# Attention, recurrence and experts on one core: the residual sum and the tile's final scaling move from VectorE to ScalarE, with new instruction orders

## The reference

```python
x = x + linear_attention(cross_attention(x, cond))         # 16 heads of 8, softmax over heads
hs = recurrence(x, h0=cond)                                # a scan over the 128 time steps
#   fused = sigmoid([x_t, h] @ w_W + w_b); a, o = split(fused)
#   h = o * h + (1 - o) * tanh(x_t @ wx + wx_b + a * (h @ wh + wh_b))
x = x + top2_of_8_experts(hs)                              # relu(h @ w1)^2 @ w2, weighted by a softmax of two logits
```

## Time and profile before

| | |
|---|---|
| median of 3 runs | 385.31 us (384.47 to 385.41) |
| the profiled execution's own time | 384.91 us |
| its span, first to last instruction | 383.2 us |
| TensorE matmuls / weight loads busy | 366.7 us (96%) / 304.8 us (80%) |
| VectorE busy | 335.3 us (88%) |
| ScalarE busy | 271.9 us (71%) |
| GpSimd busy | 261.8 us (68%) |
| granted TensorE clock, mean | 0.999 of 2.4 GHz |

### The profile page before, as it was taken

The page is one execution under the profiler, slowest core; times in us unless marked ns, Lnnn a source line. Parts: engine busy times, 40 slices in busy tenths (PEclk is TensorE's granted clock), DMA queues, the critical chain, the costliest instruction groups (busy, mean ns, idle before and its releaser), DMA issues.

```text
span 383.2 us, 9266 instructions
## 1 busy us (share of the span) xinstructions
PE 366.7 (96%) x2532; PEld 304.8 (80%) x2532; DVE 335.3 (88%) x1223; ACT 271.9 (71%) x1040; POOL 261.8 (68%) x273
## 2 busy tenths in 40 slices
PE   3899999999999999999999999999999999999985
PEld 3588788667888888888888888888888888888774
DVE  2367888999999999999999999999999999998640
ACT  2555534447788888888888887878888888776662
POOL 3799134797777777777777777777777777776000
PEclk9999999999999999999999999999999999999999
DMA  7600000000000000000000000000000000000000
GB/s 213 214 2 0 3 0 3 0 2 1 9 8 9 9 9 9 8 9 8 9 8 9 9 8 9 7 10 7 9 9 8 10 12 11 8 9 7 9 7 15
DMA packets 7585, 6.76 MB, mean 18 GB/s; under 512 B 880, under 2 KB 6256, under 8 KB 7536
## 3 DMA queue, kind: packets, MB, share of 16 engines
q1 hardware_dynamic: 7104, 5.79, 4.9%
q10 hardware_dynamic: 432, 0.39, 0.4%
HBM read 4.09 MB, written 2.10 MB: 16 GB/s over the span
## 4 chain that ended last, share of the span: by engine, by line
DVE 54%; issue 15%; PE 8%; POOL 1%; ACT 1%; DVEq 1%; POOLq 0%
DVE kvs L1072 14%; DVE att L1081 8%; PE bank L390 6%; DVE mem L1130 5%; DVE h L1150 4%; DVE bank L1135 4%; DVE rden L1064 4%; DVE bank L1142 3%; DVE kvs L1050 3%; DVE bank L1031 2%; POOL qc L347 1%; DVE bank L1104 1%; DVE bank L1056 1%; PE bank L539 1%; DVE x1T L1088 1%
## 5 line engine op out<-in xcount | busy, mean ns | idle before, releaser
L347 POOL TENSOR_TENSOR qc<-kvs,qn 128x512 f32<-128x512 f32 x64 | 81.4, 1274 | 22.9 <-DVE kvs L1072 18.8
L335 POOL TENSOR_TENSOR kv<-kv,qkv 128x512 f32<-128x512 f32 x64 | 81.1, 1268 | 2.4
L1072 DVE TENSOR_TENSOR_SCAN kvs<-bank,kv 128x256 f32<-128x256 f32 x128 | 81.5, 659 | 0.1
L390 PEld LDWEIGHTS bank<-h,gwh 128*128 128x128 f32 x512 | 68.2, 191 | 16.4 <-DVE h L1150 14.3
L832 ACT ACTIVATE hid<-bank,gw 128x128 f32<-128x128 f32 x256 | 76.3, 372 | 0.7 <-PE bank L390 0.6
L390 PE MATMUL bank<-h,gwh 128*128 128x32 f32 x512 | 72.7, 265 | 1.2 <-DVE h L1150 1.1
L390 PE MATMUL bank<-w,hsq 128*128 128x128 f32 x512 | 71.4, 283 | 1.8 <-ACT hsq L840 1.8
L390 PE MATMUL bank<-w,h 128*128 128x512 f32 x128 | 70.2, 630 | 0.0
L390 PEld LDWEIGHTS bank<-w,hsq 128*128 128x128 f32 x512 | 62.2, 192 | 3.5 <-ACT hsq L840 2.9
L858 ACT ACTIVATE gt<-bank 128x64 f32<-128x64 f32 x128 | 30.3, 237 | 44.7 <-PE bank L390 43.5
L390 PE MATMUL bank<-h,whw 128*128 128x64 f32 x256 | 50.5, 279 | 0.0
(11 more groups left out here) (112 smaller groups left out, 730.2 us busy)
## 6 DMA issues: line engine op xcount, KB each, us to landing
out_dram<-res SPq DMA_DIRECT2D x32, 64.0 KB
XT<-in_x_t_dram SPq DMA_DIRECT2D x7, 256.0 KB, 6.1
w<-in_w_dram SPq DMA_DIRECT2D x2, 512.0 KB, 5.8
XT<-in_x_t_dram ACTq DMA_DIRECT2D x1, 256.0 KB, 3.8
aw<-in_aw_dram SPq DMA_DIRECT2D x1, 192.0 KB, 3.2
gwx<-in_gw_dram SPq DMA_DIRECT2D x1, 128.0 KB, 4.6
gwh<-in_gw_dram SPq DMA_DIRECT2D x1, 128.0 KB, 4.3
cwk<-in_cwk_dram ACTq DMA_DIRECT2D x1, 64.0 KB, 1.8
```

The costliest lines, as they stand in the source:

```text
L335: pool.tensor_tensor(kv[:, a * D:b * D, :].rearrange("p (d e) h -> p d e h", d=D // 2), kv[:, D * D + a:D * D + b, :].unsqueeze(2).broadca ...
L347: pool.tensor_tensor(qc[:, a:b, :, :], kvs[:, a * D:b * D, :].rearrange("p (d e) h -> p d e h", d=D // 2), qn[:, p, a:b, :].unsqueeze(2).b ...
L390: return pe.matmul(dst, w, rhs, start=start, stop=True, skip_group_check=True)
L1072: dve.tensor_tensor_scan(flat(kvs[:, a:b, :]), scan_mask, flat(kv[:, a:b, :]), 0.0, ALU.mult, ALU.add).then_inc(kv_sum, 1)
```

## The change

`residual` becomes two ScalarE instructions: `x1_bias` writes XTt + bao into bank OUT, columns 128 to 255, TensorE's projection adds onto it, and `x1_out` copies the sum to `x1T`, now four tiles deep. The rows of x1 are no longer kept: `x_rows_out` writes them, times the sum of the weights, into OUT, columns 0 to 127; TensorE adds the experts' products there; ScalarE's `finish` multiplies by `grec` into `res`. VectorE loses `residual` and `finish`. The diff, with the ramps' lists and unchanged stretches left out (in the ramps the same calls are reordered, `x_rows` and the first experts come later, the ramp's `inverses(2, 0)` replaces VectorE's `sum_heads(2, 1)` and `residual(0)`, `sum_heads(0, *)` moves up to right after tile 0's inverses, `add_dims(0, *)` back behind `query_sum(2)`, and 34 fillers become 29):

```diff
 attT = sb("attT", [P, TOK])
-x1T = sb("x1T", [P, 2, STEPS, B])
+x1T = sb("x1T", [P, 4, STEPS, B])
...
-return (QKV, ATT)[half] if is_last(t) else HID
+return (QKV, MEM)[half] if is_last(t) else HID
...
     sp.dma_start(out_d[t], res[:, p, :]).then_inc(out_done, 16)
-for t in range(2):
-    store(t, t)
-with sp.Fori(1, TILES // 2) as it:
-    for p in range(2):
-        store(2 * it + p, p)
+for t in range(TILES):
+    store(t, t % 2)
 sp.wait_ge(out_done, 16 * TILES)
 @block.gpsimd
...
     keys(0, 0)
-    queries(0, 0)
     outer(0, 0, 0)
     outer(0, 0, 1)
+    queries(0, 0)
     weigh(0, 0, 0)
     weigh(0, 0, 1)
-    add_halves(0)
     keys(1, 1)
     outer(1, 1, 0)
-    outer(1, 1, 1)
 def iteration(t, p, has):
     q = 1 - p
+    if has(0):
+        add_halves(t)
+    if has(1):
+        outer(t + 1, q, 1)
     if has(2):
         keys(t + 2, p)
         outer(t + 2, p, 0)
...
         queries(t + 1, q)
         weigh(t + 1, q, 0)
         weigh(t + 1, q, 1)
-        add_halves(t + 1)
-    if has(2):
-        outer(t + 2, p, 1)
...
         last = mm(context_bank(u)[:, j * (D + 1) * D:(j + 1) * (D + 1) * D], pT[:, u % 2, j * P:(j + 1) * P],
-                  vbd[:, GROUP * (u % QUADS) + j, :, :].rearrange("p d h -> p (d h)"))
+                  vbd[:, GROUP * (u % QUADS) + j, :, :].rearrange("p d h -> p (d h)"), start=j == 0)
     last.then_inc(c_ps, 1)
...
     pe.wait_ge(a_red, 2 * t + 2)
-    at_least(pe, x1_done, t)
-    at_least(pe, x1t_sb, t)
+    at_least(pe, aT_sb, t)
+    at_least(pe, xr_ok, t - 2)
     pe.transpose(ATT[:, 0:P], att[:, :, :].rearrange("p h e -> p (h e)"), ident[:, :]).then_inc(aT_ps, 1)
 def project_out(t):
     pe.wait_ge(aT_sb, t + 1)
-    mm(ATT[:, P:2 * P], awo[:, :], attT[:, :]).then_inc(p_ps, 1)
+    pe.wait_ge(xb_ok, t + 1)
+    at_least(pe, xr_ok, t - 1)
+    mm(OUT[:, P:2 * P], awo[:, :], attT[:, :], start=False).then_inc(p_ps, 1)
 def x_rows(t, p):
     pe.wait_ge(x1_done, t + 1)
-    pe.transpose(ATT[:, 2 * P:3 * P], x1T[:, p, :, :].rearrange("p l b -> p (l b)"), ident[:, :])\
+    pe.wait_ge(aT_sb, min(t + 3, TILES))
+    at_least(pe, xr_ok, t)
+    pe.transpose(ATT[:, 2 * P:3 * P], x1T[:, t % 4, :, :].rearrange("p l b -> p (l b)"), ident[:, :])\
         .then_inc(x1t_ps, 1)
 def gates_x(t, p):
-    xs = x1T[:, p, :, :].rearrange("p l b -> p (l b)")
+    xs = x1T[:, t % 4, :, :].rearrange("p l b -> p (l b)")
     if isinstance(t, int) and t == 0:
         pe.wait_ge(h_init, 2)
...
     pe.wait_ge(hsq_sb, 2 * t + half + 1)
-    if half == 0 and not is_last(t):
-        at_least(pe, res_done, NE * t)
+    if half == 0:
+        pe.wait_ge(xr_ok, t + 1)
+        pe.wait_ge(x1_done, min(t + 3, TILES))
     if t == 0:
         pe.wait_ge(c_sb, 2 * QUADS)
     for j in range(4):
-        last = mm(out_bank(t)[:, 0:C], hsq[:, half, j * P:(j + 1) * P], w2[:, 4 * half + j, :],
-                  start=half == 0 and j == 0)
+        last = mm(out_bank(t)[:, 0:C], hsq[:, half, j * P:(j + 1) * P], w2[:, 4 * half + j, :], start=False)
     last.then_inc(o_ps, 1)
...
 def iteration(t, p, has):
     q = 1 - p
     if has(0):
+        gates_x(t, p)
         memory_x(t, p)
         step_gates(t, p, 0)
-        step_memory(t, p, 0)
     if has(-1):
         logits(t - 1, q)
-        hidden(t - 1, q, 0)
+    if has(0):
+        step_memory(t, p, 0)
+    if has(-2):
+        experts_out(t - 2, 0)
+        hidden_T(t - 2, 1)
+    if has(0):
+        step_gates(t, p, 1)
+        step_memory(t, p, 1)
     if has(4):
         qkv_of(t + 4)
-    if has(0):
-        step_gates(t, p, 1)
-        x_rows(t, p)
-        step_memory(t, p, 1)
-    if has(-2):
-        hidden_T(t - 2, 1)
+    if has(-1):
+        hidden(t - 1, q, 0)
+    if has(0):
+        step_gates(t, p, 2)
+        step_memory(t, p, 2)
     if has(1):
         att_T(t + 1)
-    if has(-2):
-        experts_out(t - 2, 0)
-    if has(0):
-        step_gates(t, p, 2)
-        step_memory(t, p, 2)
     if has(-2):
         experts_out(t - 2, 1)
     if has(-1):
         hidden_T(t - 1, 0)
+        x_rows(t - 1, q)
+    if has(0):
+        step_gates(t, p, 3)
+        step_memory(t, p, 3)
     if has(1):
         project_out(t + 1)
-    if has(0):
-        step_gates(t, p, 3)
-        step_memory(t, p, 3)
     if has(-1):
         hidden(t - 1, q, 1)
-    if has(1):
-        gates_x(t + 1, q)
 def finale():
+    x_rows(31, 1)
     experts_out(30, 0)
...
+def x1_bias(t):
+    if t == 0:
+        act.wait_ge(c_sb, 2 * QUADS)
+    at_least(act, res_done, t - 3)
+    act.activation(OUT[:, P:2 * P], XTt[:, STEPS * t:STEPS * (t + 1), :], ACT.Identity, bias=bao).then_inc(xb_ok, 1)
+def x1_out(t, p):
+    act.wait_ge(p_ps, t + 1)
+    at_least(act, xz_done, t - 3)
+    at_least(act, x1t_ps, t - 3)
+    act.activation(x1T[:, t % 4, :, :].rearrange("p l b -> p (l b)"), OUT[:, P:2 * P], ACT.Copy).then_inc(x1_done, 1)
 def x_rows_out(t):
     act.wait_ge(x1t_ps, t + 1)
-    act.activation(x1[:, ds(t, 1), :].rearrange("p o c -> p (o c)"), ATT[:, 2 * P:3 * P], ACT.Copy)\
-        .then_inc(x1t_sb, 1)
+    act.wait_ge(gs_done, t + 1)
+    if not is_last(t):
+        at_least(act, res_done, t)
+    act.activation(out_bank(t)[:, 0:C], ATT[:, 2 * P:3 * P], ACT.Identity, scale=gsum[:, :]).then_inc(xr_ok, 1)
+def finish(t, p):
+    act.wait_ge(o_ps, 2 * t + 2)
+    act.wait_ge(gr_done, t + 1)
+    at_least(act, out_done, 16 * (t - 1))
+    act.activation(res[:, p, :], out_bank(t)[:, 0:C], ACT.Identity, scale=grec[:, p:p + 1]).then_inc(res_done, 1)
 def relu(t, p, half, some):
...
     act.wait_ge(gw_done, t + 1)
     at_least(act, gr_done, t)
+    at_least(act, xr_ok, t)
     act.activation(gw2[:, :], gw[:, p, :], ACT.Square, accum_out=gsum[:, :]).then_inc(gs_done, 1)
 def gate_exp(t, p):
...
 def iteration(t, p, has):
     q = 1 - p
     if has(-2):
+        relu(t - 2, p, 1, 0)
+    if has(0):
+        gates(t, p, 0)
+    if has(-2):
         relu(t - 2, p, 1, 1)
     if has(0):
-        gates(t, p, 0)
+        memory_tanh(t, 0)
     if has(4):
         qkv_bias(t + 4)
-    if has(0):
-        memory_tanh(t, 0)
     if has(3):
         exp_qk(t + 3, q)
     if has(0):
         gates(t, p, 1)
-        x_rows_out(t)
+    if has(-2):
+        square(t - 2, 1)
+    if has(0):
         memory_tanh(t, 1)
+    if has(-1):
+        gate_exp(t - 1, q)
+    if has(4):
+        qkv_out(t + 4, p)
+    if has(-1):
+        relu(t - 1, q, 0, 0)
+    if has(0):
+        gates(t, p, 2)
+    if has(-1):
+        relu(t - 1, q, 0, 1)
+    if has(0):
+        memory_tanh(t, 2)
     if has(1):
         att_out(t + 1)
     if has(-1):
-        gate_exp(t - 1, q)
+        taken_sum(t - 1, q)
     if has(-2):
-        square(t - 2, 1)
+        finish(t - 2, p)
+    if has(1):
+        x1_bias(t + 1)
     if has(-1):
-        relu(t - 1, q, 0, 0)
-    if has(0):
-        gates(t, p, 2)
-    if has(-1):
-        relu(t - 1, q, 0, 1)
-    if has(0):
-        memory_tanh(t, 2)
-    if has(-1):
-        taken_sum(t - 1, q)
-    if has(4):
-        qkv_out(t + 4, p)
-    if has(-1):
-        square(t - 1, 0)
+        x_rows_out(t - 1)
     if has(0):
         gates(t, p, 3)
     if has(1):
         gates_bias(t + 1)
+        x1_out(t + 1, q)
     if has(0):
         memory_tanh(t, 3)
     if has(1):
         memory_bias(t + 1)
     if has(-1):
-        relu(t - 1, q, 1, 0)
+        square(t - 1, 0)
 def finale():
...
-def residual(t, p):
-    dve.wait_ge(p_ps, t + 1)
-    at_least(dve, x1t_ps, t - 1)
-    at_least(dve, xz_done, t - 1)
-    dve.scalar_tensor_tensor(out=x1T[:, p, :, :],
-                             in0=ATT[:, P:2 * P].rearrange("p (l b) -> p l b", b=B),
-                             scalar=bao, in1=XTt[:, ds(STEPS * t, STEPS), :],
-                             op0=ALU.add, op1=ALU.add).then_inc(x1_done, 1)
 def largest_logits(t):
     dve.wait_ge(mask_ok, 2)
...
 def taken_inverse(t, p):
     dve.wait_ge(gs_done, t + 1)
+    at_least(dve, res_done, t - 1)
     dve.reciprocal(grec[:, p:p + 1], gsum[:, :]).then_inc(gr_done, 1)
-def finish(t, p):
-    dve.wait_ge(o_ps, 2 * t + 2)
-    dve.wait_ge(gr_done, t + 1)
-    dve.wait_ge(x1t_sb, t + 1)
-    at_least(dve, out_done, 16 * (t - 1))
-    dve.scalar_tensor_tensor(out=res[:, p, :], in0=out_bank(t)[:, 0:C], scalar=grec[:, p:p + 1],
-                             in1=x1[:, ds(t, 1), :].rearrange("p o c -> p (o c)"), op0=ALU.mult,
-                             op1=ALU.add).then_inc(res_done, NE)
 def memory(t, p, s):
...
 def iteration(t, p, has):
     q = 1 - p
     if has(0):
         memory(t, p, 0)
         renewed(t, 0)
+    if has(-1):
+        drop_others(t - 1)
+    if has(0):
+        kept(t, p, 0)
+        new_h(t, p, 0)
     if has(2):
-        inverses(t + 2, 0)
-    if has(0):
-        kept(t, p, 0)
-    if has(-1):
-        largest_logits(t - 1)
-    if has(0):
-        new_h(t, p, 0)
+        sum_heads(t + 2, 1)
     if has(1):
         add_dims(t + 1, 0)
+    if has(0):
+        memory(t, p, 1)
+        renewed(t, 1)
```

(131 more changed lines are left out.)

131 lines of the change are left out of this document (58 added, 73 removed).

## The result

The changed kernel takes 383.45 us (median) against 384.48 us in the runs beside it: ratio 0.996, 95% interval 0.9949 to 0.9971. It is faster, but by 1.0 us between the medians and 1.5 by the ratio, where I forecast 6.6. One of its 11 runs took 456.13 us at a granted clock of 0.757, and the ratio is taken without it.

| stretch, by the start of the instruction that gives `x1T` | before | after | change |
|---|---|---|---|
| start to the first `x1T` | 72.94 | 71.40 | -1.5 |
| the next two tiles | 18.12 | 17.88 | -0.2 |
| 26 steady tiles | 242.46 | 241.27 | -1.2 |
| the last three | 26.46 | 27.45 | +1.0 |
| from the last `x1T` to the end | 23.2 | 22.9 | -0.3 |

The account below looks back on a forecast made before the run. VectorE was taken to pace the kernel at 9.24 us a tile, TensorE next at 9.10. 384.91 - 4.3 (steady tiles) - 1.0 (first tiles) - 1.3 (ramp) = 378.3, or 378.7 against the median; range 374.8 to 383.6.

Parts of the forecast that it names:

- What bounds the kernel now: Old steady tile: VectorE paces it at 9.24 us of its own work, with TensorE needing only 9.10.
- TensorE's 9.10 as the next bound: Steady tiles: with VectorE down to about 8.8 us, TensorE's 9.10 us of work a tile sets the pace.
- Onto ScalarE: ScalarE's queue: 0.26 us for each of three new instructions, 0.09 for a scale column, 0.87 a tile.
- the new waits: TensorE, ScalarE and VectorE queues in steady tiles: the added waits cost nothing if ScalarE's pieces have the sizes assumed.
- rival C: ScalarE's three instructions before `gates(3)` take over 1.4 us, delaying the recurrence: slower, 387.6 us at the upper bound; chance 0.07.
- the 0.6 that I had named as a sign of being wrong: ScalarE, step 3: the forecast is wrong if `gates(3)` starts over 0.6 us after its `step_gates`.
- Steady tiles: 26 steady tiles: TensorE's 9.10 plus 0.06 for late VectorE instructions, 9.16 a tile, gains 4.3 us.
- Ramp: From 40 to 76 us: the reordered ramp gains 1.3 us, between -0.5 and 3.
- first tiles: First three tiles, with fillers on TensorE: a third of VectorE's relief counts, 1.0 us, bounds 0 and 1.7.
- the rule of the Trainium skill: Add and mul belong on VectorE; set aside because in these fp32 rows ScalarE is not the slower engine.
- B: Steady tiles: TensorE as good as full, stalls VectorE hid now show, only the start gains: 382.0 us; chance 0.21.
- A: Steady tiles: TensorE is no bound, all of VectorE's 0.58 us a tile comes through: 369.3 us; chance 0.04.

Follow-up runs that it names:

- rows_late: The changed kernel with ScalarE's `x_rows_out` moved from ahead of `gates(3)` to behind `memory_bias`, after the projection: 378.64 us, 0.987 of the changed kernel.
- bias_cheap: The changed kernel with `x1_bias` reading a contiguous block of XT and adding no bias (other numbers result): 379.19 us, ratio to before 0.9858.
- late_contig: The changed kernel with `x_rows_out` after the projection, plus `x1_bias` reading a contiguous block, bias column kept (other numbers result): 377.76 us, ratio 0.9814.
- before_logits2: The kernel before, its store loop written out, with the logits product issued twice on TensorE: 390.94 us, ratio 1.0154.

## Why the prediction was wrong, by its own steps

*What bounds the kernel now.* Half right. VectorE was full, and so, in effect, was TensorE. In the old order 0.26 less of VectorE is worth 0.065 in the usual tile (0.11 on average), and 0.23 more of TensorE costs 0.24. I read 9.10 of work out of a tile of 9.24 and called the rest air; the part at step 0 was a wait for h inside the loop, which a lighter VectorE did not remove.

*TensorE's 9.10 as the next bound.* Right in sum for the new order: rows_late runs at 9.10, and a small product added there costs all of its 0.23. The parts are less good. Its steps take 2.26, 2.21, 2.16 and 2.47 against my 2.20, 2.21, 2.27 and 2.42, and its `step_gates` 0.36 to 0.41 where I had 0.36 everywhere. The errors cancel, and that 9.10 came out to the hundredth is luck. The changed kernel itself does not get there.

*Onto ScalarE, and the new waits: these steps failed.* One term was mis-sized: I charged `x1_bias` 0.26 in the queue, of bounds 0.16 to 0.59, and it measured 0.40. For its stride I had taken nothing, with 0.06 as the bound; it is 0.12. And I asked of `project_out` only whether `x1_bias` was done. Its other wait, `at_least(pe, xr_ok, t - 1)`, in `project_out(t + 1)` asks for `x_rows_out(t - 1)`, issued in the same step, last of the three, and I never named it. "More than a step old" I had said of `att_T`, `x_rows` and the experts; of `x_rows` it was false too, since its wait on `aT_sb` is for the `att_out` of the same step, but that ends at 217.39, in time for 217.71. Nor had I counted that `x_rows_out` can't start before `x_rows` has ended.

It took both errors. With `x1_bias` at the 0.26 I gave, `x_rows_out` would have waited for `x_rows` as in bias_cheap, where the wait costs 0.04 a tile and the mean is 9.158, my 9.16 (an estimate, from that run's 0.28 between the two); with the wait on that `x_rows_out` gone, an `x1_bias` of 0.40 costs nothing (rows_late, late_contig). Together they cost the 0.16. Had I only named the wait, my own sizes would have passed it, with `x_rows_out` done in the queue by 2.64 and the projection due at 2.88.

I placed the danger at `gates(3)` (rival C), with 0.2 to spare. It starts 0.62 after its `step_gates`, past the 0.6 that I had named as a sign of being wrong, but 0.61 with ScalarE idle before it (rows_late): the sign was set too tight, and the three instructions, 0.96 together instead of 0.78, held up the projection and not `gates(3)`.

*Steady tiles.* Forecast 9.16, gain 4.3 us; measured 9.280, gain 1.2. Undone by rows_late: 9.117, under the forecast, since of the 0.06 that I kept for late instructions only some 0.02 was left.

*Ramp, first tiles.* 1.3 forecast and 1.5 measured; 1.0 forecast for the first tiles and some 0.2 measured.

*The last three tiles* I had not costed at all. They lack `qkv_of`, which takes 0.70. TensorE in step 1 of the last but one of the changed kernel:

```profile
352.45 0.57 PE L385 MATMUL bank<-h,gwh 128*128 128x32 f32 x4
352.86 0.41 PE L385 MATMUL bank<-h,whw 128*128 128x64 f32 x2
353.11 1.08 PE L385 MATMUL bank<-w,h 128*128 128x512 f32 x2
354.43 0.63 PE L385 MATMUL bank<-h,gwh 128*128 128x32 f32 x4 [0.24 <-DVE h L1161]
```

Between `hidden` (353.11) and the next `step_gates` (354.43) lie 1.32 us where `hidden` needs 0.85 to 0.95; it waits for h, since 352.45 to 354.43, 1.98, is what the recurrence takes. In the new order `qkv_of` stands in a step that has nothing else to give, so the last three tiles take 9.13 to 9.18, where the old order's took 9.19, 8.86 and 8.41. I read the +1.0 in the table as that; no run tests it.

*ScalarE, and the rule of the Trainium skill.* 218.25 of 242 us is 90%, near the 92% that I gave. That add and mul belong on VectorE ("ScalarE: Activation LUTs" of the Trainium skill) is hardly borne out by the form with a scale column, 0.37 us there and 0.35 on VectorE, and is for `x1_bias`: 0.48 plus 0.28 for the copy against 0.41. My "ScalarE is not the slower one" was too strong.

*Rivals.* B's number (382.0, between 381.2 and 384.1, a mean spacing of 9.25 to 9.32) held the result. That TensorE is as good as full held too, for the old order (before_logits2). But the mean did not stay up through stalls that VectorE had hidden: late tiles became fewer, and the new order without the wait runs at 9.10. So B's number held for another reason than the one it gave. A is out: weight loads are busy 207.08 of 242.00, 86%, and the tile did not shrink by VectorE's 0.58, nor with the wait gone. C had the three instructions right, and neither the one that they hold up nor the size.

What stays open: I did not reorder the last tiles, did not take apart why the ramp gained 1.5, and have no run of the new order with the two instructions left on VectorE where they stood, so how much of rows_late's gain is the order's and how much VectorE's relief is not measured.
